# Cross attention prepared two batches ahead, with the experts' outputs gathered inside it

## The reference, cut to what matters

```
x = x + L0_xattn(layernorm(x), ctx, ctx)
x = x + L0_ffn(layernorm(x))          # top 2 of 8 experts, weighted sum of their outputs
x = x + L1_xattn(layernorm(x), ctx, ctx, mask)   # 16 heads of 16; q, k, v, softmax, Wo, bias bo
x = x + L1_ffn(layernorm(x))          # 8 heads of 64, gated, top 3
```

## Time and profile before

| what | us |
| --- | --- |
| three runs | 2660.42, 2672.16 (median), 2674.15 |
| the profiled execution: its own time | 2665.32 |
| its span, first to last instruction | 2663.6 |
| TensorE, VectorE, ScalarE, GpSimd busy | 2122.1, 1484.3, 926.3, 836.8 |
| mean granted TensorE clock | 0.937 of full |

### The profile page before, as it was taken

The page is one execution under the profiler, slowest core; times in us unless marked ns, Lnnn a source line. Parts: engine busy times, 40 slices in busy tenths (PEclk is TensorE's granted clock), DMA queues, the critical chain, the costliest instruction groups (busy, mean ns, idle before and its releaser), DMA issues. The chain is left out here.

```text
span 2663.6 us, 37640 instructions
## 1 busy us (share of the span) xinstructions
PE 2122.1 (80%) x11952; PEld 1389.3 (52%) x11961; DVE 1484.3 (56%) x2297; ACT 926.3 (35%) x1539; POOL 836.8 (31%) x753
## 2 busy tenths in 40 slices
PE   2340899999999505889888888838999999999997
PEld 1340899999999502333333333614545545554554
DVE  7820454545554344567666666544656656656655
ACT  2410333333333200455555555312333333333332
POOL 0067553435550362122212222011323323333232
PEclk9999999999999856899999999669999999999999
DMA  3162332333322332232232232324233223223322
GB/s 126 63 243 101 111 115 79 117 122 110 122 78 65 109 88 88 89 102 89 82 104 84 87 98 86 118 53 95 58 73 86 65 68 86 69 61 86 76 56 64
DMA packets 149071, 244.68 MB, mean 92 GB/s; under 512 B 22502, under 2 KB 71310, under 8 KB 146698
## 3 DMA queue, kind: packets, MB, share of 16 engines
q1 hardware_dynamic: 109762, 164.07, 21.9%
q0 software_dynamic: 11104, 44.06, 4.8%
q10 hardware_dynamic: 28160, 35.99, 4.2%
HBM read 120.48 MB, written 67.04 MB: 70 GB/s over the span
## 5 line engine op out<-in xcount | busy, mean ns | idle before, releaser
L1108 DVE TENSOR_REDUCE ca_negmax<-ca_na 128x2 f32<-128x1024 f32 x272 | 332.4, 1224 | 153.6 <-PE ca_na L901 153.6
L1020 ACT ACTIVATE ca_pr<-ca_st 128x512 f32<-128x512 f32 x512 | 278.9, 597 | 206.6 <-PE ca_st L915 205.6
L901 PE MATMUL ca_na<-ca_k_stack,ca_q_stack 64*128 64x512 f32 x544 | 222.7, 489 | 59.0 <-DMA ca_q_stack<-ca_zrow 55.6
L592 DVE TENSOR_TENSOR ex_h<-ex_up,ex_sg 128x512 f32<-128x512 f32 x136 | 94.1, 692 | 306.8 <-ACT ex_sg L555 197.4
L1706 DVE TENSOR_REDUCE sa_negmax<-sa_na 128x1 f32<-128x512 f32 x272 | 182.7, 674 | 130.8 <-PE sa_na L1527 126.5
L915 PE MATMUL ca_st<-ca_q_stack,ca_k_stack 64*128 64x512 f32 x512 | 210.6, 473 | 29.5 <-ACT ca_pr L1020 26.5
L515 PE MATMUL ex_gp<-ex_xp,moe_gu_p 128*128 128x256 f32 x1632 | 221.8, 286 | 1.4 <-DVE ex_xp L578 1.4
L515 PE MATMUL ex_up<-ex_xp,moe_gu_p 128*128 128x256 f32 x1632 | 218.4, 284 | 0.0
L528 PE MATMUL ex_yp<-moe_dn_p,ex_hp 128*128 128x256 f32 x1632 | 208.8, 286 | 11.3 <-DVE ex_hp L582 11.3
L515 PEld LDWEIGHTS ex_gp<-ex_xp,moe_gu_p 128*128 128x128 f32 x1632 | 206.1, 193 | 2.4 <-DVE ex_xp L578 1.8
L528 PEld LDWEIGHTS ex_yp<-moe_dn_p,ex_hp 128*128 128x128 f32 x1632 | 198.8, 192 | 15.2 <-DVE ex_hp L582 15.2
(11 more groups left out here) (261 smaller groups left out, 3798.1 us busy)
## 6 DMA issues: line engine op xcount, KB each, us to landing
sa_q<-sa_qh SPq DMA_DIRECT2D x140, 128.0 KB
sa_k<-sa_kh SPq DMA_DIRECT2D x140, 128.0 KB
ex_raw_m<-masks ACTq DMA_DIRECT2D x34, 512.0 KB, 3.8
moe_gu_raw<-gateupT POOLq DMA_DIRECT2D x8, 2048.0 KB, 8.2
ca_q_stack<-q_parts SPq DMA_DIRECT2D x216, 64.0 KB
ca_k_stack<-k_parts SPq DMA_DIRECT2D x216, 64.0 KB
expert_rows<-rt_zeros SPq DMA_DIRECT2D x20, 512.0 KB, 15.9
k_parts<-ca_kp SPq DMA_DIRECT2D x9, 1024.0 KB, 4.3
```

Of the source, the lines that this page charges most:

```text
L901: last = pe.matmul(na[r % 2][:, i, :], q_stack[g][rows, i, t * P:(t + 1) * P], k_stack[g][rows, i, :], start=not masked, stop=True)
L1020: act.activation(pr[:, s // HG % 2, s % HG, :], st[s % 2][:, :], ACT.Exp, scale=DK ** -0.5).then_inc(exp_done, 1)
L1108: dve.tensor_reduce(negmax[:, g % 2, 1 - r % 2, :, r // 2], na[r % 2][:, :, :], AX.X, ALU.max, negate=True).then_inc(max_done, 1)
```

## The change

`combine` is gone. In `cross_attention`:

- GpSimd gathers batches 0, 1 and 2 (8 indirect DMAs each) ahead of the loop, and batch b+3 in units 0 and 1 of batch b, into a buffer of one batch. VectorE's `absorb` does the weighting, the sum and the statistics: ahead of the loop for batches 0 to 2, in units 2 and 3 of batch b for batch b+3. The root is a power on GpSimd (`root`) and one step of Newton on VectorE (`deviation`).
- Queries and keys are made two batches ahead: k, q and xT jobs in the loop are those of batch b+2, v jobs those of b+1, and batch 1's are done between the maxima of units 0 and 1. The jobs lie in other units and runs. A second context buffer `ctxK` feeds the keys, and `nbT` has three slots.
- SyncE stores k and q of batch b+2 at the end of its loop body, after the stacks of batch b+1 have landed; then come bias, transposed bias and both contexts.
- GpSimd's queue sends the maxima into the stacks. VectorE does four of the memsets that GpSimd did, after the first queries.

```diff
-        st6, std, eps = m.sb("st6", [P, NT, 6]), m.sb("std", [P, NT]), m.sb("eps", [P, 1])
...
         wq, wk, wv, wo, bq, bk, bv, bo = (weights[n] for n in ("wq", "wk", "wv", "wo", "bq", "bk", "bv", "bo"))
+        pick = m.sb("pick", [P, TOPK, TB], U32)
...
-        JOBS = [("m", 0, 0), ("k0", 0, 1), ("n0", 0, 2), ("k1", 0, 3), ("xT0", 0, 4), ("xT1", 0, 5), ("rv", 0, 6), ("q0", 0, 7),
-                ("m", 1, 0), ("q1", 1, 1), ("t0", 1, 2), ("t1", 1, 3), ("n1", 1, 4),
-                ("m", 2, 0), ("v0", 2, 1), ("n2", 2, 2), ("v1", 2, 5),
-                ("m", 3, 0), ("n3", 3, 2), ("o0", 3, 3), ("o1", 3, 7)]
+        JOBS = [("m", 0, 0), ("n0", 0, 3), ("xT0", 0, 4), ("t0", 0, 5), ("xT1", 0, 6), ("t1", 0, 7),
+                ("m", 1, 0), ("v0", 1, 1), ("n1", 1, 2), ("o0", 1, 3), ("v1", 1, 5), ("rv", 1, 7),
+                ("m", 2, 0), ("k0", 2, 1), ("n2", 2, 2), ("o1", 2, 3), ("k1", 2, 5),
+                ("m", 3, 0), ("q0", 3, 1), ("n3", 3, 3), ("q1", 3, 5)]
         LAST = ["n0", "t0", "t1", "o0", "o1"]
-        FIRST = ["k0", "k1", "xT0", "xT1", "rv", "q0", "q1", "v0", "v1", "m"]
+        FIRST = [("k0", 0, None), ("k1", 0, None), ("v0", 0, None), ("v1", 0, None), ("rv", 0, None),
+                 ("xT0", 0, None), ("xT1", 0, None), ("q0", 0, None), ("q1", 0, None), ("xT0", 1, 2), ("xT1", 1, 3), ("rv", 1, 5), ("k0", 1, 6), ("m", 0, 7),
+                 ("k1", 1, 9), ("q0", 1, 11), ("q1", 1, 13)]
+        AHEAD = 3
...
+        def batch(name, b):
+
+            return b + 1 if name[0] == "v" else b + 2
...
+            load_context(sp, io, ctxT, ctx_in, 0)
+            for name in ("wk", "wv", "wq"):
...
+            load_context(sp, io, ctxK, ck_in, 1)
+            load_bias_T(0, 0)
+            load_bias_T(1, 1)
             load_bias(0, 0)
...
-            sp.wait_ge(misc_full, FIRST.index("v1") + 1)
-            load_context(sp, io, ctxT, ctx_in, 1)
-            send_rows(0, 0)
+            for g in range(G):
+                sp.wait_ge(stack_in[g], LOAD)
+            store(kp, k_parts, misc_free, k_stored, first("k1", 1) + 1)
+            store(qp, q_parts, qp_ready, q_stored, 2 * KC)
             with sp.Fori(0, B) as b:
                 sp.wait_ge(exp_done, b * G * SLOTS + 2)
-                for g in range(G):
-                    sp.wait_ge(stack_in[g], b * LOAD + LOAD)
-                load_bias(nxt(b), (b + 1) % 2)
-                send_rows(1, b * G + 1)
-                store(kp, k_parts, misc_free, k_stored, b * nj + (nf + number("k1") + 1))
-                send_rows(2, b * G + 2)
-                store(qp, q_parts, qp_ready, q_stored, b * KC + 2 * KC)
+                load_bias((b + 1) % B, (b + 1) % 2)
+                load_bias_T((b + 2) % B, (b + 2) % 3)
+                load_context(sp, io, ctxT, ctx_in, (b + 1) % B)
+                load_context(sp, io, ctxK, ck_in, (b + 2) % B)
...
                     load_stack(g)
-                    if g == 1:
-                        send_rows(3, b * G + 3)
-                    if g == 2:
...
+                for g in range(G):
+                    sp.wait_ge(stack_in[g], b * LOAD + 2 * LOAD)
+                store(kp, k_parts, misc_free, k_stored, b * nj + (nf + number("k1") + 1))
+                store(qp, q_parts, qp_ready, q_stored, b * KC + 3 * KC)
+            sp.wait_ge(k_stored, 16 * (B + 2))
+            sp.wait_ge(q_stored, 16 * (B + 2))
...
-                    pe.wait_ge(ctx_in, b * 16 + 16)
+                        pe.wait_ge(ck_in, b * 16)
...
+                    pe.wait_ge(ctx_in, b * 16 + 16)
...
+            pe.wait_ge(set_late, 3)
...
+            def root(b):
+
+                pool.wait_ge(mv_ready, b * TB + TB)
+                pool.tensor_tensor(wk1[:, 2, :], mv[:, :, 1], wk1[:, 3, :], ALU.add).then_inc(ve_ready, 1)
+                pool.wait_ge(ve_ready, b + 1)
+                pool.tensor_tensor(wk1[:, 0, :], wk1[:, 2, :], wk1[:, 4, :], ALU.pow).then_inc(rs_step, 1)
...
+                pool.wait_ge(ml_ready, a + 1)
+                pool.tensor_tensor(tick[:, :], ones[:, 0:1], ones[:, 0:1], ALU.mult)
+                for r in range(2):
+                    for j in range(2):
+                        row = j * HALF + RM + r
+                        pool.dma_start(q_stack[g][row:row + 1, :, :].bitcast(F32).rearrange("a i (t n) -> a (i t) n", n=P),
+                                       mrow[j * 2 * TB:(j + 1) * 2 * TB, r, :].bitcast(F32)).then_inc(m_in, 16)
...
-            pool.memset(pr[:, :, :, :], 1.0).then_inc(set_up, 1)
-            pool.memset(vw[:, :, :, :, 0:DK], 0.0).then_inc(set_up, 1)
-            pool.memset(vw[:, :, :, :, DK:32], 1.0).then_inc(set_up, 1)
-            pool.memset(on[:, :, :], 0.0).then_inc(bo_added, 1)
...
+            for b in range(2):
+                for tile in range(TB):
+                    gather(b, tile, b)
+            pool.wait_ge(wk_set, 2)
+            root(0)
             for c in range(KC):
-                split_q(c, FIRST.index(f"q{c}"), 0)
+                split_q(c, first(f"q{c}", 0), 0)
+            root(1)
+            pool.wait_ge(added, TB)
+            pool.tensor_tensor(ptick[:, 1:2], ones[:, 0:1], ones[:, 0:1], ALU.mult)
+            for tile in range(TB):
+                gather(2, tile, 0)
+            root(2)
+            pool.wait_ge(set_late, 3)
+            pool.tensor_tensor(ptick[:, 2:3], ones[:, 0:1], ones[:, 0:1], ALU.mult)
             for g in range(G - 1):
-                move_values(g, g, FIRST.index("v1"))
-            split_rows(nf - 1, 0)
-            with pool.Fori(0, B) as b:
+                move_values(g, g, first("v1", 0))
+            split_rows(first("m", 0), 0, 0)
+            for c in range(KC):
+                split_q(c, first(f"q{c}", 1), 1)
...
-                    split_rows(b * nj + (nf + [n for n, j in enumerate(JOBS) if j[0] == "m"][g]), u + 1)
+                    split_rows(b * nj + (nf + [n for n, j in enumerate(JOBS) if j[0] == "m"][g]), (g + 1) % G, u + 1)
+                        if more:
+                            pool.wait_ge(added, b * TB + AHEAD * TB)
+                            pool.wait_ge(picked, b + 1)
+                            pool.tensor_tensor(ptick[:, 0:1], ones[:, 0:1], ones[:, 0:1], ALU.mult)
                     if g == 1:
-                        split_q(1, b * nj + (nf + number("q1")), b + 1)
                         add_bias(b)
-                    if g == 0:
-                        split_q(0, b * nj + (nf + number("q0")), b + 1)
-
-                    for i in {2: (0, 1), 3: (2,)}.get(g, ()):
-                        move_values(i, u + (G - g + i), b * nj + (nf + number("v1")))
+                    if more and g < 2:
+                        for tile in (2 * g, 2 * g + 1):
+                            gather(b + AHEAD, tile, 1)
+                    if g:
+                        move_values(g - 1, u + G - 1, b * nj + (nf + number("v1")))
+                    if g == 3:
+                        for c in range(KC):
+                            split_q(c, b * nj + (nf + number(f"q{c}")), b + 2)
+                        if more:
+                            root(b + AHEAD)
...
+
+                    if step < 2:
...
+                            dve.wait_ge(gathered[i], count)
+                        dve.scalar_tensor_tensor(out=x[:, one(t), :], in0=got[i][:, tile, step, :], scalar=weight[:, step, one(t)],
+                                                 in1=x[:, one(t), :], op0=ALU.mult, op1=ALU.add).then_inc(added if step else first_in, 1)
...
+                            dve.wait_ge(added, t + len(tiles))
+                        dve.bn_stats(st6[:, tile, :], x[:, one(t), :]).then_inc(st_ready, 1)
...
+                            dve.wait_ge(st_ready, t + len(tiles))
+                        dve.bn_aggr(mv[:, tile, :], st6[:, tile, :]).then_inc(mv_ready, 1)
...
+            def deviation(b):
+                dve.wait_ge(rs_step, b * 5 + 1)
+                dve.tensor_tensor(z, y, y, ALU.mult).then_inc(rs_step, 1)
...
+                dve.wait_ge(rs_step, b * 5 + 4)
+                dve.tensor_tensor(rstd[:, :], y, z, ALU.mult).then_inc(rs_step, 1)
...
+            for n, (name, b, spot) in enumerate(FIRST):
+                if name == "xT0" and b == 0:
+                    for step in range(4):
+                        absorb(0, step, None, 0, 16 * TOPK * TB)
+                    deviation(0)
+                    normalise(0, 0)
...
+            dve.memset(pr[:, :, :, :], 1.0).then_inc(set_late, 1)
+            dve.memset(vw[:, :, :, :, 0:DK], 0.0).then_inc(set_late, 1)
...
+            dve.memset(on[:, :, :], 0.0).then_inc(bo_added, 1)
+            for step in range(4):
+                absorb(1, step, None, 1, 16 * TOPK * TB)
+            deviation(1)
+            normalise(1, 1)
+            for step in range(4):
+                absorb(2, step, None, 0, 2 * 16 * TOPK * TB)
+            deviation(2)
...
-            with dve.Fori(0, B) as b:
+                    for n, (name, b, spot) in enumerate(FIRST):
```

(63 more changed lines are left out.)

171 lines of the change are left out of this document (72 added, 99 removed).

## The result

The changed kernel takes **2585.75 us** (median of 4 runs, 2583.95 to 2590.56) against 2673.02 of the kernel before on the same chip (4 runs, 2660.42 to 2674.15): a ratio of 0.9684, 95% interval 0.9656 to 0.9712. The forecast was 2598, with a range from 2549 to 2632. The profiled execution took 2590.56, the longest of the four.

The account below looks back on a forecast made before the run. TensorE was taken to set the loop's pace, with a stack wait in each batch, and GpSimd's gathers the pace ahead of it: 2665.3 - 50 - 68.8 + 31.5 + 9.8 + 8 + 2.3 = 2598 us, range 2549 to 2632.

Parts of the forecast that it names:

- The head, -50: Ahead of the loop: the new chain starts the loop at 1024 instead of 1074, -50 us (-42 to -57).
- The stack's wait and its half clock, -68.8: Unit 2 of each batch: TensorE's stack wait and slow clock behind it go, 8.6 us eight times.
- 6.2 + 2.4: Per batch in unit 2: 6.2 us of pause plus 2.4 of half clock, giving a batch of 66.5.
- The context, +31.5: v0 in unit 1, run 1: context late behind stores and biases on SyncE's queue, 4 x 5.1 + 3 x 3.7 us.
- The clock, +9.8: Behind each of seven context pauses: slower TensorE clock costs 1.4 us, 9.8 in all (0 to 17).
- VectorE and GpSimd, +8: Loop: VectorE's added work mostly hidden, 1.3 x 5, plus 0.2 a batch for normalisations; GpSimd's added DMAs cost nothing.
- GpSimd's split of q1 and the power, about 1 us: Loop: VectorE's last added piece waits about 1 us for these, in part hidden.
- The root itself: Head, after absorb(0): root and deviation, six tiny instructions at 0.15 to 0.45 us each, 2.0 taken.
- The end, +2.3: End of the stage: SyncE's last stores finish behind the last addition to `x`, delaying the next block 2.3 us.
- Context in time: Rival, loop: the context is not late, by faster transfers or longer unit 0; 2557 us, chance 0.27.
- The wait for the maxima's DMAs: Rival, each unit's first transposed score: maxima late by GpSimd's queue, kernel slower, 2710 at 3.5 us each; chance 0.05.
- VectorE did not become the bound: Rival, loop and head: VectorE's extra work and waits for GpSimd show in full, 2629 us; chance 0.14.

Follow-up runs that it names:

- root first: Changed kernel with GpSimd's root moved ahead of the split of q1 instead of behind it: 2586.53 us, ratio 0.97.
- early context: Changed kernel with the value's context loaded two batches ahead, right behind the third stack: 2540.48 us, ratio 0.9525.
- best order: Changed kernel with context two batches ahead, root before q1's split, third got buffer, batch 2's gathers behind root(0): 2520.21 us, ratio 0.9444.
- the last pair: Context two batches ahead, third got buffer, batch 2's gathers behind root(0); root ahead of q1's split 2520.21 us, behind both splits 2528.40 us.
- root last: The 2520.21 us kernel with the root left behind both splits of q, as in the changed kernel: 2528.40 us, ratio 0.9476.
- third buffer: Changed kernel with a third got buffer, so batch 2's gathers follow at once on those of batch 1: 2577.13 us, ratio 0.9633.

## Why the prediction was right, and where its terms were off

The mechanism held: the stack's wait went, the context became late in its place seven times, with half clock behind it, and the head shrank as worked out. Several sizes were off, and that the total came so near (2598 against 2590.6 in the profiled execution, 2585.8 by the median) is partly luck. The next block begins 81.8 earlier (1610.30 against 1692.10, its first load), where the terms of the sum make 67.2. Seven of this were lost again in the self attention, whose code is the same: 978.5 from there to the end against 971.5. In the kernels with the root first, with the early context and with the best order it took 972.1, 975.3 and 976.8, so it moves by some us between executions; what moves it stays open.

- **The head, -50.** The first score of the loop is 51.5 earlier, but by two errors that cancel. TensorE's start (917 forecast, 917.75 measured), absorb(0) (937; 937.70) and xT0 (945.3; 946.64) came as worked out, and the first score at 975.16 for 974.8. The gathers of batch 2, taken with 12.1 from issue to landing, took 15.5 (971.28 to 986.74) beside the loads of the stacks, so the maxima began at 994.20 and not 989.8. From there to the loop it was 28.5, not 34.4: of the 14 chosen for batch 1's jobs 8.1 showed, and the rest lay beside the maxima.
- **The stack's wait and its half clock, -68.8.** All gone. But a batch without a late context is not 66.5 but 64.0. The step "6.2 + 2.4" counted only the pause and what follows it (and took the score of 0.49 with the pause, whose wait is 5.78). The jobs, spread anew over the runs, also cut the wait of the transposed scores for ScalarE's exponentials from 26.5 (55 times) to 14.0 (30 times), and the kernel with the combine block of before and the loop of after has the same 14.0, so it is the order that does this:

```profile
PE ca_st L925 <- ACT ca_pr L1036: 14.0, 30, 0.7
```

  This is the largest error, some 20 us over eight batches, more than the 14.6 that the forecast of the stage missed in all. These waits explain 12.5 of it; the rest stays open.
- **The context, +31.5.** Measured 31.3. The single waits, 3.7 to 5.0, agree with 3.7 and 5.1; but not where they fall: 5.1 was forecast for the batches with gathers, where 3.91 to 4.81 were measured, and 3.7 for those without, where 3.72, 4.91 and 4.97 were. The gathers do delay the load: from the first store to the context's landing pass 13.6 to 13.9 us in the four batches with gathers and 12.5 to 12.7 in the three without (forecast 12.9 and 11.5). But TensorE, too, comes to v0 later in them, 9.0 to 9.7 us behind that store against 7.7 to 8.8, so the waits are no longer. That the total agrees to 0.2 is luck.
- **The clock, +9.8.** 14.0, by the medians of the run without the wait (12.3 in the v jobs alone); inside the bounds of 0 to 17, nearer the upper one, the price of the pause of 5.8.
- **VectorE and GpSimd, +8.** With the context early, seven batches stand 10.6 us over seven of the shortest (63.8 us). Of these some 7 are the root, as the last pair shows (8.2 by the medians, 7.1 by the loops). The chain "GpSimd's split of q1 and the power, about 1 us" was 1.5, and it did not hide.
- **The root itself**, bounded at 0.15 to 0.45 by tiny instructions: the power took 1.05 (the four steps of deviation 0.16 each). Root and deviation together took 2.1 (942.96 to 945.07), where the sum had chosen 2.0.
- **The end, +2.3.** The last stores were issued at 1602.71 and 1603.21, the last addition to `x` began at 1608.71 and the next block 1.6 behind it, against 1.2 before; so about 0.4 and not 2.3. (The forecast's own numbers, 16.7 less 14.1, make 2.6.)
- **The rivals.** Context in time did not happen, and the run that made it so gave 2540, not 2557: it, too, was priced from a batch of 66.5, with the price of the clock at 1.4 a wait. The wait for the maxima's DMAs did not come: they took 0.53 each and not the 1.3 of the gathers, 2.16 for four. VectorE did not become the bound (53 of 64 to 73).

## What to carry to other kernels

When a transfer is moved to an earlier stage of a queue, write down what now stands ahead of every other load on that queue, and ask for each when its reader comes: here 45 us, two thirds of the 69 that the forecast gave for the stack's wait, went to the next load behind, and issuing it earlier gave them back. An edit that brings nothing may only lengthen another wait by what it saves (root first gave 0 with the context late, 1.4 with the context early while VectorE's unnamed pauses stood in the loop, and 8 once both were gone); try it again when the other waits are gone. And a shorter wait can be worth more than its length: cutting the context's waits by 20.1 us, from 31.3 to 11.2, gained 36.6, since the half clock behind most of them went too.

## What was not expected of the hardware

- GpSimd's power of two small tiles (128x4) takes 1.05 us, a sum or product of the same size 0.20:

```profile
942.96 0.20 POOL L1003 TENSOR_TENSOR ca_wk<-ca_mv,ca_wk 128x4 f32<-128x4 f32 x1 [16.82 <-DVE ca_mv L1132]
943.24 1.05 POOL L1005 TENSOR_TENSOR ca_wk<-ca_wk 128x4 f32<-128x4 f32 x1
```

- Pauses of TensorE from 3.7 to 5.0 us were followed by 1.2 GHz seven times of seven, those of 0.8 to 2.1 twice of seven (in other runs one of 2.05 and one of 3.00 were, too); and in unit 0 of the kernel with the root last even three short waits in a row (0.35, 0.60 and 0.43 us, from 1075.7 to 1078.2) were followed by half clock, 1.93 for a sum of values that takes 1.06, where the same unit with the root first, with 0.35 and 0.59, kept 1.00.
- Direct DMAs issued by GpSimd took 0.53 each, indirect ones 0.95 with 0.3 between:

```profile
1092.11 2.16 POOL L1030 DMA_DIRECT2D ca_q_stack<-ca_mrow  x4
```

- With 24 gathers in one row VectorE stood idle for 8.1 and 10.1 us ahead of one instruction (some 2 of them while TensorE still wrote its input) until about the time when they had landed; with 16, and 8 more later, it did not. Such waits, named "remote", were also in the loops of two kernels with the early context and root first, 10.9 us in the one without the third buffer and 14.5 in the one with it, and once, 2.0, in that with the third buffer alone. The loop with the 14.5 has the very code of the best kernel, which has none. What the traces show is their place: each of the thirteen in the loops ends 0.8 to 1.2 us after GpSimd has issued the last gather of that unit, and the two in the head 3.1 and 3.8 us after the last of the 24. Whether VectorE's code, an unrecorded semaphore or a memory port was late was not tried and stays open.
